# Second attention layer: the first maximum product of a step issued ahead of the last score product

## What is computed

```
x = x + L0(_gn(x))
# L1, on _gn(x):
qkv = x @ qkv_w.T + qkv_b          # q, k, v: (B * 12, 2304, 32)
attn = (q * scale) @ k.T + rel_h[..., :, None] + rel_w[..., None, :]
attn = softmax(attn, axis=-1)
out = (attn @ v) @ proj_w.T + proj_b
x = x + out
```

## Time and profile before

| what | value |
|---|---|
| median of 3 runs | 3285.41 us (3283.49 to 3287.42) |
| the profiled execution, its own time | 3281.58 us |
| its span, first to last instruction | 3279.3 us |
| mean granted TensorE clock | 0.941 |
| PE busy | 2889.2 us, 88% |
| DVE busy | 2484.8 us, 76% |
| POOL busy | 1903.4 us, 58% |
| ACT busy | 1864.8 us, 57% |
| one reduction of a maximum piece on VectorE (L1715), mean | 556 ns |
| one `low_part` on GpSimd (L1704), mean | 1467 ns |

### The profile page before, as it was taken

The page is one execution under the profiler, slowest core; times in us unless marked ns, Lnnn a source line. Parts: engine busy times, 40 slices in busy tenths (PEclk is TensorE's granted clock), DMA queues, the critical chain, the costliest instruction groups (busy, mean ns, idle before and its releaser), DMA issues. The chain is left out here.

```text
span 3279.3 us, 94851 instructions
## 1 busy us (share of the span) xinstructions
PE 2889.2 (88%) x34200; PEld 1920.0 (59%) x34200; DVE 2484.8 (76%) x5171; ACT 1864.8 (57%) x3434; POOL 1903.4 (58%) x1561
## 2 busy tenths in 40 slices
PE   1996999997379766999999999999999999999977
PEld 1553677774245543666666666666666666666654
DVE  6744788885765545888888888888888888888854
ACT  3333667674333433666666666666666666666655
POOL 3452555551212103777777777777777777777762
PEclk9996999998689657999999999999999999999989
DMA  2426555656222697222222222222222222223114
GB/s 118 174 88 145 132 134 141 143 134 208 104 90 87 171 210 205 51 51 51 52 51 52 51 51 51 51 51 51 51 51 51 51 51 51 54 62 63 29 41 145
DMA packets 162461, 294.95 MB, mean 90 GB/s; under 512 B 78522, under 2 KB 112404, under 8 KB 156564
## 3 DMA queue, kind: packets, MB, share of 16 engines
q1 hardware_dynamic: 162052, 289.43, 34.7%
HBM read 189.37 MB, written 85.45 MB: 84 GB/s over the span
## 5 line engine op out<-in xcount | busy, mean ns | idle before, releaser
L1704 POOL TENSOR_TENSOR fprob_low<-fprob 128x768 f16<-128x768 f32 x1008 | 1449.8, 1467 | 487.1 <-ACT fprob L1672 487.0
L1715 DVE TENSOR_REDUCE fpart_max<-fmax_acc 128x1 f32<-128x384 f32 x2592 | 1354.6, 556 | 301.5 <-PE fmax_acc L1543 285.6
L1672 ACT ACTIVATE fprob<-fscores 128x768 f32<-128x768 f32 x1296 | 1049.1, 810 | 640.7 <-PE fscores L1572 640.6
L1543 PE MATMUL fmax_acc<-fk_m,fq_m 128*128 128x384 f16 x2592 | 850.8, 329 | 39.5 <-DMA fident<-in_ident 34.7
L1570 PE MATMUL fscores<-fq_a,fk_a 128*128 128x384 f16 x2592 | 847.6, 327 | 40.0 <-issue 30.8
L1572 PE MATMUL fscores<-fq_b,fk_b 97*128 97x384 f16 x2592 | 850.9, 328 | 8.8 <-issue 8.8
L1596 PE MATMUL fout_acc<-fv,fprob 128*128 128x65 f16 x7776 | 611.7, 191 | 2.5 <-POOL fprob_low L1704 2.1
L1597 PE MATMUL fout_acc<-fv,fprob_low 128*128 128x33 f16 x7776 | 595.8, 179 | 2.5 <-issue 2.5
L1596 PEld LDWEIGHTS fout_acc<-fv,fprob 128*128 128x128 bf16 x7776 | 542.7, 97 | 78.8 <-POOL fprob_low L1704 5.2
L1597 PEld LDWEIGHTS fout_acc<-fv,fprob_low 128*128 128x128 f16 x7776 | 487.1, 96 | 61.7 <-issue 4.1
L1089 POOL TENSOR_TENSOR prob_low<-prob 128x242 f16<-128x242 f32 (+2 forms) x360 | 250.0, 716 | 256.4 <-ACT prob L1047 255.6
(11 more groups left out here) (128 smaller groups left out, 3822.5 us busy)
## 6 DMA issues: line engine op xcount, KB each, us to landing
q_a<-q_hi SPq DMA_DIRECT2D x48, 432.0 KB, 5.7
fq_a<-q_hi SPq DMA_DIRECT2D x48, 432.0 KB, 7.7
q_a<-q_lo SPq DMA_DIRECT2D x24, 432.0 KB, 7.4
row_bias<-x SPq DMA_DIRECT2D x24, 432.0 KB, 7.8
col_bias<-x SPq DMA_DIRECT2D x72, 144.0 KB, 3.9
fq_a<-q_lo SPq DMA_DIRECT2D x24, 432.0 KB, 8.5
fq_a<-col_bias SPq DMA_DIRECT2D x24, 432.0 KB, 12.0
fq_b<-row_bias SPq DMA_DIRECT2D x24, 432.0 KB, 14.9
```

The lines of the kernel that those rows point to most:

```text
L1543: nc.tensor.matmul(max_acc[:, piece_bank(g, u, j), 0:PIECE], q_m[:, b, tile * 128:(tile + 1) * 128], k_m[:, b, piece * PIECE:(piece + 1) * ...
L1672: nc.scalar.activation(prob[:, k % RING, :].rearrange("p (j n) -> p j n", j=2), scores[:, 2 * (k % 2):2 * (k % 2) + 2, 0:UNIT], ACT.Exp).t ...
L1704: engine.tensor_tensor(prob_low[:, k % RING, :], prob[:, k % RING, :], prob[:, k % RING, :].bitcast(BF16)[:, 1::2], ALU.subtract).then_inc ...
L1715: nc.vector.reduce_max(part_max[:, u % 2, j // PIECES, j % PIECES:j % PIECES + 1], max_acc[:, piece_bank(g, u, j), 0:PIECE], axis=AX.X).th ...
```

## The change

`scores_of` is split. `scores_begun` issues the two score products of tile 0 and the first one of tile 1; `scores_ended` issues the second product of tile 1, which raises `score_ready`. `max_piece(..., 0)` stands between the two. No instruction is added or removed, no wait is changed, and the orders of VectorE, ScalarE, GpSimd and SyncE stay as they were.

```diff
--- before.py
+++ after.py
@@ -1557,7 +1557,8 @@
                                             start=True, stop=True)
                 last.then_inc(row_ready, 1)
 
-            def scores_of(n, b, p):
+            def scores_begun(n, b, p):
+
 
                 a, k = p // PAIRS, p % PAIRS
                 if k == 0:
@@ -1569,9 +1570,16 @@
                     bank = scores[:, 2 * (p % 2) + j, 0:UNIT]
                     nc.tensor.matmul(bank, k_a[:, b, tile * 128:(tile + 1) * 128],
                                      q_a[:, b, tile // NA, a * UNIT:(a + 1) * UNIT], start=True, stop=False)
-                    last = nc.tensor.matmul(bank, k_b[:, tile % NA], q_b[:, b, a * UNIT:(a + 1) * UNIT],
-                                            start=False, stop=True)
-                last.then_inc(score_ready, 1)
+                    if j == 0:
+                        nc.tensor.matmul(bank, k_b[:, tile % NA], q_b[:, b, a * UNIT:(a + 1) * UNIT],
+                                         start=False, stop=True)
+
+            def scores_ended(b, p):
+
+
+                a, tile = p // PAIRS, 2 * (p % PAIRS) + 1
+                nc.tensor.matmul(scores[:, 2 * (p % 2) + 1, 0:UNIT], k_b[:, tile % NA],
+                                 q_b[:, b, a * UNIT:(a + 1) * UNIT], start=False, stop=True).then_inc(score_ready, 1)
 
             def weighted(n, b, p):
 
@@ -1613,13 +1621,14 @@
                     coming = row_of(n, k)
                     if coming:
                         row_of_max(*coming)
-                    scores_of(n, b, k)
+                    scores_begun(n, b, k)
                     if k + AHEAD == STEPS and not is_last(n):
                         pe.wait_ge(max_in[1 - b], (h + 1 + b) * MAX)
                     later = ahead(n, k)
                     side = b if k + AHEAD < STEPS else 1 - b
                     if later:
                         max_piece(later[0], side, later[1], 0)
+                    scores_ended(b, k)
                     if k >= LAG:
                         weighted(n, b, k - LAG)
                     elif not is_first(n):
```

## The result

The changed kernel takes 3316.95 us, the median of 4 runs (3314.64 to 3322.64), against 3284.45 us for the kernel before in 4 runs (3281.64 to 3287.42). The ratio is 1.0101, 95% interval 1.0084 to 1.0119: 1.0% slower. Forecast were 3335 us and a range of 3316 to 3350. The way is right and the size too large: 50 us slower were forecast, 32.5 us were measured. The measured time lies within the range by 1 us only, and outside the narrower 3325 to 3345 that the forecast gave for itself.

The account below looks back on a forecast made before the run. TensorE and VectorE hand the bound to each other within a unit. Per unit 0.165 + 0.165 + 0.05 = 0.38 us, for 144 units 54.7, less 3.8 and about 0.5, leaves 50: 3285.4 + 50 = 3335 us, range 3316 to 3350.

Parts of the forecast that it names:

- VectorE's two chains of 2.31 us begin at max1 and an earlier max0 doesn't shorten them: From second maximum product of steps 7 and 3 to first of steps 0 and 5: VectorE's pace, unchanged at 2.31 us.
- 0.165 us behind each of the two places: Behind the first maximum products of steps 0 and 5, one more score product: 0.51 becomes 0.675 us, +0.33 per unit.
- 0.05 us for low(3) beside GpSimd: VectorE's low part of step 3 meets GpSimd's later run and ends later: +0.05 us per unit, between nothing and 0.18.
- The tie at the weighted sum of step 1: TensorE issues it 4.37 us after step 0's first maximum product; GpSimd allows it at 4.36: costed at nothing.
- The piece max1(5) to row begins at a max1 as well and contains only VectorE's links, so it stays 1.80 us: From step 5's second maximum product to the next row: VectorE's pace, no change, costed at nothing.
- A row sooner than 1.80 us behind max1(5): Sign that the forecast is wrong: the row comes sooner than 1.80 us after step 5's second maximum product.
- the rival in which only one place grows: Only step 0's or step 5's wait grows, or part is absorbed: 3307 us, chance 0.08.
- 0.33 to 0.40 us per unit: Growth per unit behind the forecast's own range, given as 3325 to 3345 us.
- The rival by which the chain begins at max0: An earlier first maximum product starts VectorE's low part of step 3 or 7 up to 0.165 us earlier: 3262 us, chance 0.04.
- the GpSimd rival: GpSimd becomes a bound, delaying step 1's weighted sum or costing 0.18 at the low part: about 3350 at 0.1 us, chance 0.12.
- The fetches at the loop's start: In 10 loop iterations, instruction fetches ahead of steps 0 and 5 swallow the stalls and their growth: 3.8 us off.
- The clock: Rival: more short stalls lower TensorE's granted clock from 0.99; at 0.94, 86 us more, 3421 us; chance 0.02, within slower.

Follow-up runs that it names:

- the kernel with steps 3 and 7: Against the kernel before, in steps 3 and 7 first maximum product behind two score products, second between halves of the weighted sum: 3261.52 us, ratio 0.9925.
- step 5 alone: Against the kernel before, first maximum product moved ahead of the last score product in step 5 only: 3308.35 us, ratio 1.0078.
- the doubled advance: Against the kernel before, first maximum product moved two score products earlier instead of one, in step 5 only: 3327.95 us, ratio 1.0132.
- the late score in steps 0 and 5: Against the kernel before, half the weighted sum swapped with the last score product in steps 0 and 5, maximum products unmoved: 3316.52 us, ratio 1.0086.
- step 6 alone: Against the kernel before, first maximum product moved ahead of the last score product in step 6 only: 3270.76 us, ratio 0.9947.
- the late score in step 5: Against the kernel before, half the weighted sum swapped with the last score product in step 5 only, maximum products unmoved: 3298.07 us, ratio 1.0041.
- the kernel with steps 3, 6 and 7: Against the kernel before, steps 3 and 7 with both maximum products earlier, plus step 6's first maximum product ahead of its last score product: 3257.94 us, ratio 0.9921.

## Why the prediction was right in its sign and too high in its size

The two places and their price were right, and one term was missing, a gain at the row. With the measured 13.06 us in place of 13.18 the same sum gives 3318 us.

- **VectorE's two chains of 2.31 us begin at max1 and an earlier max0 doesn't shorten them**: right. 2.31 us after, and it holds at step 5 with max0 two places ahead. Moving max1 is another matter: in the kernel with steps 3 and 7 both chains begin earlier, and part of that arrives at max0.
- **0.165 us behind each of the two places**: right, by the change (0.51 to 0.68 twice), by step 5 alone (0.17) and by the doubled advance (0.33). It is the order behind the waiting product that costs, and no fixed price of an exchange.
- **0.05 us for low(3) beside GpSimd**: right, 1.00 instead of 0.95 us and 2.36 instead of 2.31.
- **The tie at the weighted sum of step 1**: held in the change. That it was close, and that GpSimd's hold-up has a price of its own where the 0.165 us doesn't cover it, the late score in steps 0 and 5 showed: 0.14 us in step 2.
- **"The piece max1(5) to row begins at a max1 as well and contains only VectorE's links, so it stays 1.80 us"**: this step failed. The link from fneg_max to the reduction of max0(6) was 0.23 us before, of which 0.13 was VectorE waiting for TensorE's max0(6). The exchange in step 6 removed it: 1.66 us, -0.14 per unit, which step 6 alone shows as 12.81 to 12.68. In my sum a gain of up to 0.165 stood as nothing, though the same paragraph gave that bound. 144 x 0.13 is 19 us, and the forecast was 18 us too high. A row sooner than 1.80 us behind max1(5) was named there as a sign that the forecast is wrong, and it came.
- **The range**: that it holds the result is luck. Its lower end came from the rival in which only one place grows, not from the gain at the row; that gain at its full bound would have gone to 3311. And 0.33 to 0.40 us per unit give 3329 to 3339, not the 3325 to 3345 that stand beside them.
- **The rivals**: the time lies between the forecast and the half-sized rival, and only the pieces tell that it isn't that one: both places grew by 0.17. The rival by which the chain begins at max0 is out by the 2.31 us, and the GpSimd rival by the tie and the 0.05.
- **The fetches at the loop's start**: their places were right, and 3.8 us were taken off for them. The runs don't show that term: the distances add to 58 us more than 134 steady units after and 54.8 before, so the length of the waits hides it. That this length moves by more than 10 us in total between kernels with the same number of instructions wasn't foreseen. It limits what medians tell here; the steady unit tells 0.02 us.
- **The clock**: 0.99 granted from 1400 to 3100 us before and after; the rival didn't occur. By the earlier trace rows TensorE's busy time in a unit was 12.2 us, not 12.1, which changes nothing.

Open is what sets the length of the fetches, and whether the kernel with steps 3, 6 and 7 could keep both gains with an earlier max1(6), whose reading holds max0(7). Neither was tried.

## What to carry to other kernels

The change makes the distances between maximum products nearly equal (0.51 and 0.82 us became 0.68 and 0.65 behind max0(0)), and that is worth nothing by itself. Ask for each place where the in-order producer waits which chain releases it and where that chain begins: an operation moved ahead of its release only takes the work behind it into the wait, and one that heads the releasing chain gains when it is moved ahead, until another chain ends later. When a link looks like one engine's own, check its start against the other engine's last product plus the usual delay (0.36 us here), since a wait under the record in front, like the 0.13 us here, isn't printed. And when the forecast itself bounds a gain, put the bound into the range.

## What was not expected of the hardware

- A VectorE reduction can follow a small reduction (fneg_max, 0.18 us) after 0.10 us; 0.23 us in the kernel before was the wait for a product.
- VectorE's low part, begun while GpSimd was in its run, ended 0.81 to 0.82 us behind GpSimd's end both when the two met for 0.19 us (1.00 us long) and when they met for 0.66 us (1.48 us long).
- The first products of a loop iteration waited for nothing visible for 3.4 us on average in the kernel before and 4.8 us with the late score in step 5 (30.8 and 43.1 us in 9 starts), with the same number of instructions in the loop. Over all 14 traces the wait has two lengths, about 3.5 and about 4.8 us.
